# Moving the second LayerNorm of a tile pair from the middle of the pair to its end in an eight-core attention and FFN kernel

## The reference

```python
x = x + _L0_attn_ref(_layernorm(x, axis=-1), ...)
x = x + _L0_ffn_ref(_layernorm(x, axis=-1), ...)     # the "second LayerNorm"

# the ffn, h of width 1024, weights dequantised, plus a rank-32 side path each
h = x
for blk in range(3):
    y = _qlora_linear(h, qweights[2*blk], ...)
    y = _layernorm(y, ln_gamma[blk], ln_beta[blk])
    y = jax.nn.gelu(y, approximate=False)
    y = _qlora_linear(y, qweights[2*blk+1], ...)
    h = y + h
```

## Time and profile before

| | us |
|---|---|
| median of the runs of the kernel before (4132.85 and 4140.03) | 4136.44 |
| the profiled execution | 4173.68 |
| its span on core 3, the slowest | 4172.2 |
| its fastest core (4) | 4120.5 |
| phase B on core 3, from the first L1243 at 2189.67 to the end | 1982.5 |

### The profile page before, as it was taken

How to read it: one execution, slowest core, us unless ns; L and a number is a source line. 1 busy time by engine, 2 the same in 40 slices (tenths; PEclk the granted TensorE clock), 3 DMA queues, 4 the chain that set the end, 5 groups by cost and what they waited for, 6 DMA issues and landing times.

```text
span 4172.2 us, 57543 instructions; the slowest of 8 cores (4120.5 to 4172.2 us)
## 1 busy us (share of the span) xinstructions
PE 2546.0 (61%) x20176; PEld 1609.6 (39%) x20176; DVE 1982.1 (48%) x3863; ACT 1009.4 (24%) x1729; POOL 77.0 (2%) x126
## 2 busy tenths in 40 slices
PE   0466666566656666666437657565665766657666
PEld 0344443344444433444104434343443434434343
DVE  0455544454555544554335545445453444544444
ACT  0122233322222333322461212122121211211121
POOL 1000000000000000000020000000000000000000
PEclk9766766677767766676558878778886777777777
DMA  9011111121111112112230010201001010010101
GB/s 136 13 32 29 30 28 29 29 34 29 29 34 32 24 29 34 29 29 39 56 111 6 6 46 1 51 1 42 9 6 46 1 51 1 13 38 1 46 1 31
DMA packets 259705, 128.18 MB, mean 31 GB/s; under 512 B 229232, under 2 KB 233504, under 8 KB 259424
## 3 DMA queue, kind: packets, MB, share of 16 engines
q1 hardware_dynamic: 228864, 79.72, 9.4%
q0 software_dynamic: 30560, 44.79, 5.8%
HBM read 61.99 MB, written 25.17 MB: 21 GB/s over the span
## 4 chain that ended last, share of the span: by engine, by line
PE 45%; DVE 24%; ACT 11%; issue 9%; DMA 5%; another core or an unknown queue 2%; DVEq 2%; SPq 1%; ACTq 1%; POOL 0%; POOLq 0%
PE psA L1275 11%; PE psB L1452 5%; PE psA L1452 5%; DMA arena<-arena 4%; ACT arena L795 3%; PE psA L773 3%; ACT arena L1409 2%; PE psA L385 2%; PE psA L1281 2%; DVE arena L1356 2%; PE psA L460 2%; DVE arena L807 2%; PE psB L892 2%; ACT L1364 1%
## 5 line engine op out<-in xcount | busy, mean ns | idle before, releaser
L1275 PE MATMUL psA<-arena,wbig 128*128 128x256 bf16 x3072 | 481.4, 309 | 0.4 <-DVEq L1304 0.2
L773 PE MATMUL psA<-arena 64*128 64x256 bf16 x960 | 249.7, 391 | 170.3 <-ACT arena L795 170.3
L1275 PEld LDWEIGHTS psA<-arena,wbig 128*128 128x128 bf16 x3072 | 301.2, 108 | 123.2 <-issue 31.5
L1364 ACT ACT_TABLE_LOAD x48 | 61.6, 1283 | 1064.4 <-DVEq L1357 1064.4
L807 DVE TENSOR_TENSOR arena<-arena,mlocS 128x512 bf16<-128x512 bf16 x480 | 204.1, 425 | 228.2 <-ACT arena L795 204.5
L1301 DVE TENSOR_SCALAR arena<-psA,biasS 128x256 bf16<-128x256 f32 x384 | 185.9, 484 | 257.6 <-PE psA L1281 214.5
L795 ACT ACTIVATE arena<-psA 128x512 bf16<-128x512 f32 x480 | 260.9, 594 | 59.9 <-PE psA L773 58.8
L1452 PE MATMUL psA<-arena,wbig 128*128 128x256 bf16 x1536 | 232.2, 302 | 0.0
L1424 PE MATMUL psC<-arena,laS 128*32 128x256 bf16 x384 | 70.5, 346 | 258.3 <-ACT arena L1409 258.3
L385 PE MATMUL psA<-wbig,arena 128*128 128x512 bf16 x512 | 137.2, 430 | 135.0 <-DMA arena<-arena 125.5
L1452 PE MATMUL psB<-arena,wbig 128*128 128x256 bf16 x1536 | 210.9, 283 | 0.0
(11 more groups left out here) (166 smaller groups left out, 4355.0 us busy)
## 6 DMA issues: line engine op xcount, KB each, us to landing
y<-arena SPq DMA_DIRECT2D x16, 1024.0 KB, 4.4
arena<-qT POOLq DMA_DIRECT2D x48, 256.0 KB, 2.6
arena<-x_in POOLq DMA_DIRECT2D x16, 512.0 KB, 6.6
x2scr<-arena SPq DMA_DIRECT2D x16, 512.0 KB, 3.0
arena<-x2scr POOLq DMA_DIRECT2D x16, 512.0 KB, 6.2
arena<-arena SPq DMA_TRANSPOSE x224, 3.2
wbig<-wq POOLq DMA_DIRECT2D x1, 2048.0 KB, 18.7
wbig<-wk POOLq DMA_DIRECT2D x1, 2048.0 KB, 30.4
```

The lines of the kernel that those rows point to most:

```text
L773: mm = t.matmul(reg[:, hh * 256:(hh + 1) * 256], ar_t.ap()[0:64, o_KR + h * 2 * W + sl * W + koff: o_KR + h * 2 * W + sl * W + koff + 128] ...
L1275: t.matmul(reg, wTv(i0, c, oc * 128, 128), V(hin_o + c * TILE, TILE), start=(c == 0), stop=False)
L1364: I(sc, s.activation(br(TILE, TILE), sr(2 * TILE, TILE), AF.Sqrt))
```

## The change

`emit_ln2(2 * pair + 2)` is moved from the middle of the pair (k = 1) to behind `b_tail(Bst)`, directly ahead of the `emit_h0(2 * pair + 2)` that uses it. The load `emit_x2load(2 * pair + 2)` stays where it is. Nothing is added or removed: the same instructions run, 7 times in all (pairs 0 to 6), at another place of the VectorE and ScalarE queues.

```diff
                 if k == 1 and 2 * pair + 2 < nbt_total:
                     emit_x2load(2 * pair + 2)
-                    emit_ln2(2 * pair + 2)
                 b_Ga(A, k)
                 b_Y2(A, k)
                 b_E2(A, k)
@@
             b_tail(Bst)
             if 2 * pair + 2 < nbt_total:
+                emit_ln2(2 * pair + 2)
                 emit_h0(2 * pair + 2)
             if 2 * pair + 3 < nbt_total:
                 emit_x2load(2 * pair + 3)
```

## The result

| | before | changed |
|---|---|---|
| median of the runs, us | 4139.07 (10 runs) | 4077.86 (11 runs) |
| lowest run | 4132.74 | 4064.05 |
| ratio to before, 95% interval | | 0.9853 [0.9812, 0.9893] |
| slowest core of the profiled execution, span | 4172.2 | 4064.9 |

The changed kernel is 1.5% faster, within the 2% that count as no change here. The forecast was 4066 us, 70.5 us less than before. Between the medians it is 61 us. Between these medians it is 70 us.

A forecast was written before the change was run, and what follows sets the result against it. TensorE was taken to be held by waits for Gelu in A1 and for h0 transposes at pair starts. From the 4136.4 us median, 86.3 gained less 15.8 paid gave 4066 us, range 4045 to 4098 (own range 4054 to 4080).

The forecast's parts named there:

- The sum: Whole kernel: 86.3 us gained less 15.8 paid, 70.5 us off the 4136.4 us median, giving 4066 us.
- Step 1: Half A1: removing emit_ln2 at k = 1 ends TensorE's 12.91 us wait for Gelu, gaining 7 x 12.33 = 86.3 us.
- Step 2: Pair boundary: inserted emit_ln2 makes each L1133-to-L1243 stretch 11.3 us, 79.1 against 63.3 in all, costing 15.8 us.
- Step 3: Queues behind the moved work: tile B's transposes still land in time, so its first L1243 shows no wait; no cost.
- a chain without slack: Pair boundary before the change: tail transposes, add, y store, x2 load, h0 transposes, L1243 in order, TensorE idle 18.43 us.
- Transposes slow by their own form: Rival, pair boundary: h0 transposes stay at 8.8 us, boundaries cost 44.8 us, time 4095 us; chance 0.14.
- The clock that takes it back: Rival, whole pairs: closing the stall slows TensorE's clock, about 12 us per pair, time 4150 us; chance 0.06.
- The run without slowed stretches: Rival, whole run: slowest core does as well as core 4 before, 4120.5 - 70.5 = 4050 us; chance 0.14.
- The price by the page on table loads: Pair boundary, ScalarE: the page's estimate adds 1.38 us of drain per boundary, 9.7 us in all; the forecast added none.

The follow-up runs named there:

- experiment 1: Kernel before with emit_ln2(2p+2) left out at both places, so seven tiles lack their second LayerNorm: 4042.8 us, ratio 0.9769.
- experiment 3: Kernel before with tile B's y store issued after the next h0 transposes land: 4113.1 us; with the x2 load held back too: 4128.0 us.
- experiment 4: Kernel before with x2 load after the h0 transposes: 4123.8 us; with y store later too and transposes waiting for the tail's add: 4148.8 us.
- experiments 2 to 4: Kernel before with emit_ln2(2p+2) at k = 1 cut in three, square roots behind A1's Gelu: 4137.5 us; plus experiment 3 and experiment 4.
- experiments 1, 5 and 6: experiment 1; kernel before, emit_ln2(2p+2) in A0: 4048.1 us; changed kernel, it and emit_h0 in B2: 4034.8 us, tail's add also deferred: 4000.1 us.

## Why the prediction was right

**The sum.** 4066 us was forecast with a range of 4045 to 4098, and the medians are 4078 and 4070. Undisturbed runs differ by 4138.5 - 4068.5 = 70 us, where the sum had 70.5. That it came this close is in part luck: the profiles give about 3 us less on either side, 83.4 us gained and 12.6 paid.

**Step 1.** The stall went whole, with Gelu done 0.8 to 2.0 us before TensorE asked for it, where 0.6 was worked out. The price had come from pair 7 of before, which already ran without `emit_ln2` at k = 1. The five intervals from A0 to B2, summed over seven pairs, are 1186.7 us on core 5 of before and 1103.3 on core 2 of after: 83.4 us gained where 86.3 were forecast. The removal alone gained 88 us in them on the mean of the cores (cores 4 to 7 of before), and 94 to 96 in all. So the term holds for the five intervals it was read from. What it left out is 5 to 6 us at the boundaries, where the matmuls ran at a higher granted clock (experiment 1). The changed kernel does not have them: its matmuls around the wait took 331.1 us at 0.87 on core 2.

**Step 2.** From the first L1133 to L1243 the seven boundaries took 11.36, 11.32, 11.24, 11.41, 11.74, 11.27 and 11.29 us, together 79.6, forecast 79.1. The transposes took 4.7 to 4.9 us, forecast 4.9. Against 63.3 us before that is 16.3 us. Over the whole boundary intervals it is only 539.3 - 526.7 = 12.6 us paid: most of the rest came back in the matmuls around the wait (331.1 us against 334.3 on core 5 of before). Against a kernel with no LayerNorm at either place the new place costs 23 us, more than the 15.8 of the sum, and the old one 94, more than the 86.3; in the difference of the two the shortfalls cancel.

**Step 3.** Tile B's first L1243 showed no wait: the eight waits of L1243 above are those of the eight tiles A.

**What was wrong in the argument.** I called the boundary of the kernel before a chain without slack. It was not: experiment 3 showed the h0 transposes ready and held only by the y store ahead of them in SyncE's queue. The error did not touch the sum, because the store stayed where it was. It matters for what could be gained: I weighed two places for `emit_ln2` and never asked what else the boundary's 18 us were made of.

**The rivals.** Transposes slow by their own form: fell in experiment 4.

The clock that takes it back: it moved the other way. The mean granted clock from the first L1375 to the last was 0.807 to 0.813 on cores 4 to 7 of before, and 0.825 to 0.830 on all cores of the changed kernel. Of the runs with clocks on record, four or more cores were below 0.742 in 20 of 40 of before, 6 of 16 of the changed kernel, 16 of 32 in experiments 2 to 4, and 1 of 16 in experiments 1, 5 and 6, the kernels with the least idle. There is no sign that closing the stall brings it on.

The slower stretch from which I priced this rival has nothing to do with the pause. The 0.81 of pair 3 in the earlier trace rows is a mean of 0.50 and 1.00. From 3175 to 4162 us cores 2 and 3 of before have stretches in which a busy TensorE is granted 0.81 throughout, a third level between the two; pairs 4 and 6, with 259 and 255 us, lie there. A window of core 3, columns as in the earlier trace rows:

```profile
3241.00:3266.00 25.00, 22.74 (x150) 14.21 (x150) 10.28 (x21) 4.43 (x9) 0.00 (x0) 0.81 0.00 1
```

Cores 0 and 1 have the same from 133 to 1136 us, in phase A, where the kernels do not differ; cores 4 to 7, with the same stall in every pair, never do, and neither does any core in the two profiles of the changed kernel. What starts such stretches stays open. The page "TensorE: Matmul & The Clock Gate" of the Trainium skill, in its note on the peak-current limiter in part 1, has the whole die go to 13/16 of the clock once three of its cores run dense matmuls, for as long as the load lasts. The level agrees with the 0.81 here. The condition does not cover it: all eight cores run this program, and the level came to some pairs of cores and not to others, and not more often in the denser kernel.

The run without slowed stretches, at 4050 us: single cores ended as early as 4048.2, but the slowest of eight did not come below 4064. The summed stretch is alike on all cores of the changed kernel, within 5 us; what spreads is where phase B begins, with the first L1375 at 2213.1 us on core 5 and 2227.7 on core 2, whose spans are 12.4 us apart.

**The price by the page on table loads.** ScalarE's load at L1150 took 1.28 us in the new place too and hid beside the second statistics, and the square root began 0.01 us behind it (2419.86 + 1.28 = 2421.14, and 2421.15). Six of the seven new chains of 11.2 to 11.4 us leave no room for a further 1.38 us each, which the estimate from the Trainium skill's "ScalarE: Activation LUTs", under "What ACT_TABLE_LOAD costs", would have added.

## What to carry to other kernels

Ask of a piece of work not how long it is but who stands behind it in each queue that it uses: the same LayerNorm cost 94 us in A1, 23 at the pair's end and nothing that shows in A0, where TensorE was waiting for ScalarE anyway. If the last piece of a loop already runs as the edit would have it, its row gives a price before anything is built, but only for the stretch that it covers. And before a wait is called a chain, look whether the waiting transfer's inputs have long been ready: a store that waits for its own data holds every transfer behind it in the queue of the engine that issues it.

## What the hardware showed

- Two SBUF-to-SBUF DMA transposes of 128x1024 bf16 release their reader after 4.7 us alone, 6.4 us beside a 1024 KB store to DRAM and 8.5 us beside that and a 512 KB load on GpSimd's queue (medians over all cores, experiment 4 and before).
- A pause of TensorE costs more than its length. In a wait of 5.80 us the granted clock fell to 0.50, and the next three groups of eight matmuls of 256 columns, with their side-path matmuls, took 5.62 us; behind a wait of 1.44 us, at 1.00, they took 3.57 us.
- Beside 0.50 and 1.00 there is a granted clock of 0.81 on a busy TensorE. In the profile of before it came in stretches spread over some 1000 us to cores 2 and 3 in phase B and to cores 0 and 1 in phase A, while the other die ran the same program without it.
